# Extra constant products on TensorE in four waits of a one-core decoder, and one gather two batches earlier in its queue

## The chip, the core and the metric

One core of a Trainium2 chip runs the whole program. The metric is the device time of one execution in microseconds (us); smaller is better. Engines are named as in the profile: PE (TensorE, PEld its weight loads), DVE (VectorE), ACT (ScalarE), POOL (GpSimd), SP (SyncE, which issues DMAs).

## The reference

A two-layer decoder on 32 sequences of 128 tokens with 128 features. Every sublayer is followed by a residual sum and a layer norm.

```
layer 0: attention + MLP, cross-attention, a mixture of 8 experts (top 2)
layer 1: x4 = norm(x3 + experts)         # joined at the start of the decode phase
         x5 = norm(x4 + causal attention with rotary embedding (16 heads of 8))
         for t in 0..127:                # gated recurrence over the context
             r = decay * r + k[t] * v[t];   inp = (q[t] * r) @ Wi.T + bi
             gate = sigmoid(inp @ Wg.T + bg)
             state = tanh((gate * state + (1 - gate) * inp) @ A.T + inp @ Bm.T)
             out[t] = state @ Wo.T + bo
         x6 = norm(x5 + out);   x7 = norm(x6 + one of 8 experts (512 hidden, gelu))
```

## The kernel before, in words

The program is a row of phases, each a block in which every engine has its own instruction list; all engines meet in a barrier between two phases. Order between engines inside a phase is made by semaphores alone. Each list is written by a loop over ticks; `due(tick, offset)` says for which batch a step falls on this tick. Each engine runs its list in order, so a step that waits holds back all that stands behind it on its engine.

**`phase_decode`** (812 to about 1126 us of the span) runs ticks -25 to 148, four per batch (one per group of four heads, 128 units in all). For batch b, POOL gathers two expert rows by indirect DMA (L1574, `gather`), DVE joins them with x3 (L1797, L1832, on tick 4b-17) and takes mean and variance, POOL makes the reciprocal root (L1599), DVE makes x4 (L1840, tick 4b-13), PE transposes x4 (L1699, tick 4b-10), ACT copies it (L1744), PE projects q and k (L1679, tick 4b-8) and v, DVE multiplies with the rotary table (L1788), POOL adds and spreads (L1583, L1586, tick 4b-6), PE makes the scores (L1626, tick 4b-1), and on ticks 4b to 4b+3 DVE takes the maximum and subtracts it (L1771, L1775). ACT exponentiates, PE transposes into the bank `turned` (L1635) and weighs. At the end, on tick 4b+19, PE transposes x5 (L1714) and ACT copies it into `xT_all` (L1749).

POOL runs `gather(b)` on tick 4b-25, except `gather(4)`, which runs on tick -5, ahead of `gather(5)` and behind the rotary steps of batch 0. From b = 4 on, a gather waits until batch b-4 has been joined.

**`phase_recurrent`** (about 1127 to 1280 us) runs ticks -23 to 175. The 128 steps are cut into 16 spans of 8. For each span PE makes three products of 256 columns and more (L2038 input, L2042 gate, L2047 and L2050 drive), for span 0 on ticks -13, -10, -6 and -5. Per step there is a loop: PE product of 32 columns (L2008), ACT tanh (L2072), DVE product with the gate (L2130), back to PE. Every fourth tick a line of four steps goes on: three products (L2018, L2020, L2023), statistics, POOL's root, ACT x6 (L2091), transpose (L2014), logits (L2032), and for four lines the counts (L2055 to L2058). After the last line POOL scatters the last eight lines to memory (L1970) and DVE makes the tile table (L473 to L498).

**`phase_last`** (from about 1280 us) runs 40 tiles of 128 sorted rows: SP loads rows (L2264) and expert weights (L2272), PE transposes the rows (L2312), makes the hidden product (L2305) and the down product (L2320).

Of the kernel before, what the change touches and what calls it, by code (L numbers as in the profile page):

```python
# [14 lines left out]
P = 128  # L15
# [72 lines left out]
def stand_alone(eng, c):  # L88


    eng.sem_inc(c["stood"], 1)


def load_function(nc, c, function):
# [508 lines left out]
def phase_encode(nc, c, d, scr, keep, experts0, table0):  # L603

    with Phase(nc) as ctx:
# [6 lines left out]
        def bank(name):  # L612
# [3 lines left out]
        turned_bank, mix_bank, vec_bank, act_bank = bank("turned"), bank("mix"), bank("vec"), bank("act")  # L616
# [25 lines left out]
        scores_done, max_ready, bank_read, probs_ready, probs_turned, probs_t_ready, mixed, mix_copied = (  # L642
            sem("scores_done"), sem("max_ready"), sem("bank_read"), sem("probs_ready"), sem("probs_turned"),
            sem("probs_t_ready"), sem("mixed"), sem("mix_copied"))
# [111 lines left out]
        def _(pe):  # L756
# [58 lines left out]
            for tick in ENCODE_TICKS:  # L815
# [103 lines left out]
                if (i := group_at(tick, 69)) is not None:  # L919
# [8 lines left out]
                        if s < size:  # L928
                            nc.tensor.matmul(out, lhsT=c["tri"][:], rhs=r["any"][:, s, :], start=s == 0, stop=True)
                    last.then_inc(vec_written, 1)  # L930

        @block.scalar
        def _(act):
            def read(name, n):
# [500 lines left out]
def due(tick, offset):  # L1435

    n, rest = divmod(tick - offset, G)
    return n if rest == 0 and 0 <= n < BATCH else None


UNITS_ALL = BATCH * G


STEPS = 8
SPANS = P // STEPS
# [56 lines left out]
def phase_decode(nc, c, d, keep, scr, xT_all, experts1, recur):  # L1502
# [4 lines left out]
    with Phase(nc) as ctx:  # L1507
# [61 lines left out]
        def _(pool):  # L1569
            def gather(b):  # L1570
                if b >= 4:
                    pool.wait_ge(joined4, b - 3)
                for q in range(2):
                    nc.gpsimd.indirect_dma_start(out=y[q][b % 4][:], out_offset=None, in_=scr["expert_out0"],  # L1574
                                                 in_offset=bass.IndirectOffsetOnAxis(ap=route["out_rows"][:, b, q:q + 1], axis=0))\
                        .then_inc(gathered[b % 4], 16)

            for tick in TICKS:
# [21 lines left out]
                        .then_inc(rstd4_ready, 1)  # L1600
                if (b := due(tick, -26)) is not None and b in (12, 22):
                    pool.drain()
                if tick == -5:
                    gather(4)
                if (b := due(tick, -25)) is not None and b != 4:
                    gather(b)
                if tick == 104:
                    pool.drain()
# [7 lines left out]
        def _(pe):  # L1616
# [37 lines left out]
            for tick in TICKS:  # L1654
# [60 lines left out]
                if (n := due(tick, 7)) is not None:  # L1715
                    pe.wait_ge(mix_copied, n + 1)
                    if n:
                        pe.wait_ge(joined5, n)
                    else:
                        pe.wait_ge(halves_ready, 4)  # L1720
                    for k in range(G):
                        last = nc.tensor.transpose(vec_bank[:, k * P:(k + 1) * P], ot[n % 2][:, k * P:(k + 1) * P], c["ident"][:])
                    last.then_inc(mix_back, 1)

        @block.scalar
        def _(act):
# [150 lines left out]
def phase_recurrent(nc, c, d, scr, keep, e, xT_all, experts1):  # L1877
# [5 lines left out]
    with Phase(nc) as ctx:  # L1883
# [118 lines left out]
        def _(pe):  # L2002
            pe.wait_ge(e["loaded"], RECUR_LOADS)
            for tick in TICKS_RECUR:
# [47 lines left out]
                if (i := quad_at(tick, 32)) is not None:  # L2052
                    pe.wait_ge(hot_ready, i + 1)
                    at_votes = votes[:, COUNTED].rearrange("p (s e) -> p s e", e=EXPERTS)
                    nc.tensor.matmul(at_votes, lhsT=c["tri"][:], rhs=hot[:, 1:SLOTS + 2, :], start=True, stop=False)  # L2055
                    nc.tensor.matmul(at_votes, lhsT=c["ones"][:], rhs=hot[:, 0:SLOTS + 1, :], start=False, stop=False)
                    for s in range(2, SLOTS + 1):
                        last = nc.tensor.matmul(at_votes[:, s:SLOTS + 1, :], lhsT=c["ones"][:], rhs=hot[:, 1:SLOTS + 2 - s, :],  # L2058
                                                start=False, stop=s == SLOTS)
                    last.then_inc(counted, 1)  # L2060

        @block.scalar
        def _(act):
# [153 lines left out]
def phase_last(nc, c, d, keep, kept, e, sorted_rows, out, loaded):  # L2217
# [3 lines left out]
    with Phase(nc) as ctx:  # L2221
# [73 lines left out]
        def _(pe):  # L2295
            expert_of, experts = loader(pe, "down", "tile_expert", EXPERTS - 1), {}
            pe.wait_ge(keep["experts_loaded"], loaded)
            for tick in TICKS:
                if 0 <= (n := tick) < tiles:
                    pe.wait_ge(rowsT_ready, n + 1)  # L2300
# [193 lines left out]
```

## Time and profile before

| | |
|---|---|
| median of 3 runs | 1378.81 us (1376.04 to 1379.27) |
| the profiled execution | 1374.22 us, its span 1372.4 us |
| mean granted TensorE clock | 0.941 of full |
| busy | PE 87%, DVE 76%, ACT 63%, POOL 40% |

The rows further down are times from the start of the span. "PEclk" is the share of TensorE's full clock that was granted: 1.00 is 2.4 GHz and 0.50 is 1.2 GHz. Queue names such as SPq are the engine's issue of DMAs.

### The profile page before, as it was taken

Reading aid. Unit: us, or ns where it says so; the run is one execution under the profiler, and the core shown is the slowest. Engines: PE = TensorE matmul, PEld = TensorE weight load, DVE = VectorE, ACT = ScalarE, POOL = GpSimd, SP = SyncE. Lnnn points to the kernel's source line nnn. Section 1 sums busy time; section 2 is a strip of 40 time slices with the busy share of each in tenths; the row PEclk is TensorE's granted clock in tenths of the full one; section 3 lists DMA queues with packets and bytes.
Section 4 is the critical chain, followed back from the end, with each engine's and each line's share of the span. In section 5 each row is a group of like instructions: output and inputs, shape, how many; then the busy total and the mean of one; then the engine's idle time right before and its main releaser. Section 6 shows DMA issues by size and latency. Waiting matters only on the chain. (4 is left out here: it accounts for less than half of the span.)

```text
span 1372.4 us, 31512 instructions
## 1 busy us (share of the span) xinstructions
PE 1190.9 (87%) x10024; PEld 806.6 (59%) x10024; DVE 1042.1 (76%) x3169; ACT 863.6 (63%) x2470; POOL 552.7 (40%) x830
## 2 busy tenths in 40 slices
PE   3889999999999999988399977999999969997696
PEld 2456666666666666654266644555555537766696
DVE  3467888887888888876678867999999974665465
ACT  2578887878887878864256633666666654443464
POOL 1133333425353434442400026555556311556377
PEclk9899999999999999998599987999999988997798
DMA  6100000000000000000122222013100000000673
GB/s 267 50 15 11 17 15 21 29 17 27 16 30 17 28 17 17 15 13 13 56 71 82 82 66 95 23 38 94 28 24 19 1 3 1 17 17 21 180 209 90
DMA packets 71488, 63.51 MB, mean 46 GB/s; under 512 B 10510, under 2 KB 61586, under 8 KB 70688
## 3 DMA queue, kind: packets, MB, share of 16 engines
q1 hardware_dynamic: 63344, 46.33, 11.5%
q0 software_dynamic: 6400, 12.63, 2.9%
q10 hardware_dynamic: 1584, 2.54, 0.5%
q8 instruction: 85, 1.39, 0.4%
q14 instruction: 75, 0.61, 0.1%
HBM read 43.00 MB, written 18.98 MB: 45 GB/s over the span
## 5 line engine op out<-in xcount | busy, mean ns | idle before, releaser
L762 PE MATMUL e_bank_turned<-c_matrices,e_probs 128*128 128x128 f32 x1024 | 166.1, 286 | 16.0 <-ACT e_probs_t L995 8.7
L688 POOL TENSOR_TENSOR e_rstd<-e_var_eps,c_minus_half 128x1 f32<-128x1 f32 x128 | 70.7, 576 | 252.5 <-DVE e_var_eps L1036 252.2
L995 ACT ACTIVATE e_probs_t<-e_bank_turned 128x512 f32<-128x512 f32 x256 | 155.0, 605 | 16.1 <-PE e_bank_turned L762 14.6
L1123 DVE TENSOR_REDUCE e_neg_max<-e_bank_scores 128x4 f32<-128x512 f32 x160 | 109.6, 685 | 50.1 <-PE e_bank_scores L805 49.6
L762 PEld LDWEIGHTS e_bank_turned<-c_matrices,e_probs 128*128 128x128 f32 x1024 | 116.6, 145 | 39.8 <-issue 16.0
L772 PE MATMUL e_bank_mix<-e_probs_t,e_values 128*32 128x128 f32 x2048 | 113.6, 296 | 15.3 <-ACT e_probs_t L995 14.8
L954 ACT ACTIVATE e_probs<-e_scores,e_neg_max 128x128 f32<-128x128 f32 x384 | 123.3, 411 | 1.2 <-DVE e_neg_max L1159 1.2
L1752 ACT ACTIVATE d_probs_t<-d_bank_turned 128x512 f32<-128x512 f32 x128 | 77.4, 604 | 64.0 <-PE d_bank_turned L1635 64.0
L691 POOL TENSOR_TENSOR e_k_by_place<-e_q_k_k,c_matrices 128x512 f32<-128x512 f32 x64 | 66.6, 1040 | 105.3 <-DVE e_q_k_k L1167 105.3
L949 ACT ACTIVATE e_probs<-e_scores 128x512 f32<-128x512 f32 x128 | 82.1, 642 | 42.2 <-DVE e_scores L1156 41.6
L1734 ACT ACTIVATE d_probs<-d_scores 128x512 f32<-128x512 f32 x128 | 80.8, 631 | 42.4 <-DVE d_scores L1775 42.2
L1635 PE MATMUL d_bank_turned<-c_matrices,d_probs 128*128 128x128 f32 x512 | 82.2, 284 | 26.3 <-ACT d_probs_t L1752 21.3
L1635 PEld LDWEIGHTS d_bank_turned<-c_matrices,d_probs 128*128 128x128 f32 x512 | 55.5, 141 | 62.2 <-issue 53.5
L1775 DVE TENSOR_TENSOR d_scores<-d_bank_scores,d_neg_max 128x512 f32<-128x512 f32 x128 | 88.5, 692 | 4.4
L1156 DVE TENSOR_TENSOR e_scores<-e_bank_scores,e_neg_max 128x512 f32<-128x512 f32 x128 | 88.3, 690 | 3.4
L1771 DVE TENSOR_REDUCE d_neg_max<-d_bank_scores 128x4 f32<-128x512 f32 x128 | 87.5, 683 | 3.6 <-PE d_bank_scores L1626 3.6
L1574 POOL DMA_INDIRECT d_first<-scratch_expert_out,keep_out_rows x32 | 32.1, 1003 | 137.6 <-POOLq L85 131.7
L772 PEld LDWEIGHTS e_bank_mix<-e_probs_t,e_values 128*32 128x32 f32 x2048 | 41.2, 110 | 63.5 <-issue 34.4
L1325 PE MATMUL m_wide<-up,m_rowsT 128*128 x144 | 76.2, 612 | 0.4 <-ACT m_rowsT L1390 0.4
L699 POOL DMA_INDIRECT scratch_sorted<-e_x,e_row_u x64 | 64.2, 1003 | 26.8 <-issue 14.3
L2072 ACT ACTIVATE n_states<-n_bank_drive 128x32 f32<-128x32 f32 x128 | 25.2, 197 | 69.8 <-PE n_bank_drive L2008 68.4
L1125 DVE TENSOR_TENSOR e_scores<-e_bank_scores,c_bias 128x512 f32<-128x512 f32 x96 | 65.7, 684 | 0.0
(322 smaller groups left out, 3238.0 us busy)
## 6 DMA issues: line engine op xcount, KB each, us to landing
streamed<-in_s_up SPq DMA_DIRECT2D x40, 258.0 KB, 2.9
m_rows<-scratch_sorted SPq DMA_DIRECT2D x72, 64.0 KB, 1.8
scratch_expert_out<-m_y SPq DMA_DIRECT2D x72, 64.0 KB, 1.5
f_rows<-scratch_sorted SPq DMA_DIRECT2D x40, 65.0 KB, 2.5
e_x_in<-in_x SPq DMA_DIRECT2D x32, 64.0 KB, 1.8
e_ctx_in<-in_ctx SPq DMA_DIRECT2D x32, 64.0 KB, 2.1
up<-in_m_wgv SPq DMA_DIRECT2D x1, 2048.0 KB, 7.7
up_b<-in_m_bgv SPq DMA_DIRECT2D x1, 2048.0 KB, 14.3
```

The lines of the kernel that those rows point to most:

```text
L762: last = nc.tensor.transpose(turned_bank[:, j * P:(j + 1) * P], pr[k % 3][:, j, :], c["ident"][:])
L772: last = nc.tensor.matmul(mix_bank[32 * j:32 * j + VC, g * P:(g + 1) * P], lhsT=va[att][n % 3][:, G * g + j, :], rhs=pt[k % 2][:, j * P:(j ...
L949: nc.scalar.activation(pr[k % 3][:], sc[k % 4][:], ACT.Exp).then_inc(probs_ready, 1)
L954: last = nc.scalar.activation(pr[k % 3][:, j, :], src[:, j, :], ACT.Exp, bias=nmax[k % 4][:, j:j + 1], scale=1.0)
L995: nc.scalar.activation(pt[k % 2][:], turned_bank[:], ACT.Copy).then_inc(probs_t_ready, 1)
L1123: nc.vector.tensor_reduce(nmax[k % 4][:], bank, AX.X, ALU.max, negate=True).then_inc(max_ready, 1)
L1156: nc.vector.tensor_tensor(sc[k % 4][:], bank, bcast(nmax[k % 4][:], P), ALU.add).then_inc(bank_read, 1)
L1635: last = nc.tensor.transpose(turned_bank[:, j * P:(j + 1) * P], pr[u % 3][:, j, :], c["ident"][:])
L1734: nc.scalar.activation(pr[tick % 3][:], sc[tick % 4][:], ACT.Exp).then_inc(probs_ready, 1)
L1752: nc.scalar.activation(pt[(tick - 1) % 2][:], turned_bank[:], ACT.Copy).then_inc(probs_t_ready, 1)
L1771: nc.vector.tensor_reduce(nmax[tick % 4][:], bank, AX.X, ALU.max, negate=True).then_inc(max_ready, 1)
L1775: nc.vector.tensor_tensor(sc[tick % 4][:], bank, bcast(nmax[tick % 4][:], P), ALU.add).then_inc(shifted, 1)
```

## The change

A helper `stream` multiplies the constant identity with the first columns of a constant weight matrix (fp32, as many columns as its output has) into a part of PSUM whose contents nobody needs. It signals nothing and waits for nothing. It is called on PE

- in the decode phase on ticks -21 to -5 (17 calls of 256 columns), and on ticks 132 to 148 (17 calls of 128 columns), ahead of which PE waits for the last copy out of the bank `turned`;
- in the recurrence on ticks -12, -11, -9 and -4 (128 columns), and from tick 114 to tick 175 (62 calls of 128 columns), ahead of which PE waits for the last gate;
- in the last phase three times with 512 columns ahead of the first tile.

Each call stands behind the other PE steps of its tick. Besides, POOL's `gather(4)` moves from tick -5 to tick -9, its place by the rule of the other batches.

```diff
+def stream(nc, c, out):
+    nc.tensor.matmul(out, lhsT=c["ident"][:], rhs=c["a_w1"][:, 0:out.shape[1]], start=True, stop=True)
...
-                if tick == -5:
-                    gather(4)
-                if (b := due(tick, -25)) is not None and b != 4:
+                if (b := due(tick, -25)) is not None:
                     gather(b)
...
+                if -21 <= tick < -4:
+                    stream(nc, c, turned_bank[:, 0:2 * P])
+                if tick == UNITS_ALL + 4:
+                    pe.wait_ge(probs_t_ready, UNITS_ALL)
+                if UNITS_ALL + 4 <= tick:
+                    stream(nc, c, turned_bank[:, 0:P])
...
+                if tick in (-12, -11, -9, -4):
+                    stream(nc, c, turned[:, 0:P])
+                if tick == P - STEPS - 6:
+                    pe.wait_ge(gate_ready, SPANS)
+                if tick >= P - STEPS - 6:
+                    stream(nc, c, front[:, 0:P])
...
             pe.wait_ge(keep["experts_loaded"], loaded)
+            for _ in range(3):
+                stream(nc, c, sums[1][:])
```

## Rows read from the trace of the kernel before

**Rows 1.** The page, section 2: granted clock in 40 equal slices.

```profile
PEclk9899999999999999998599987999999988997798
```

**Rows 2.** Windows: length, busy by PE, PEld, DVE, ACT, POOL, granted clock, DMA, GB/s.

```profile
812.00:832.50 20.50, 12.21 (x44) 7.94 (x45) 9.78 (x33) 1.39 (x5) 15.64 (x20) 0.50 0.21 58
...
1122.60:1143.10 20.50, 14.68 (x41) 10.72 (x42) 8.65 (x35) 5.12 (x18) 1.79 (x3) 0.50 0.01 3
1143.10:1252.30 109.20, 102.79 (x620) 75.32 (x618) 69.61 (x328) 52.75 (x232) 52.89 (x112) 1.00 0.04 13
1252.30:1286.40 34.10, 15.00 (x68) 13.04 (x69) 12.29 (x60) 7.93 (x31) 16.14 (x25) 0.50 0.33 90
```

**Rows 3.** Timeline of the decoder's fill: start, duration, engine, line, operation, count, idle before.

```profile
814.61 1.89 PE L1619 MATMUL d_bank_scores<-c_causal_bf,c_ident_bf 128*128 128x512 bf16 x4 [5.61 <-DVE d_values L1762]
...
820.25 0.48 PE L1699 MATMUL d_bank_act<-c_matrices,d_x 128*128 128x128 f32 x1 [3.75 <-DVE d_x L1840]
...
825.08 0.57 POOL L1599 TENSOR_TENSOR d_rstd<-d_var_eps,c_minus_half 128x1 f32<-128x1 f32 x1
825.62 0.71 POOL L1583 TENSOR_TENSOR d_q_k_rotated<-d_halves 128x256 f32<-128x256 f32 x1
...
826.42 1.06 POOL L1586 TENSOR_TENSOR d_k_by_place<-d_q_k_rotated,c_matrices 128x512 f32<-128x512 f32 x1
...
827.96 0.46 POOL L1596 TENSOR_TENSOR d_x_bo<-d_x,c_rows 128x128 f32<-128x128 f32 x1 [0.48 <-DVE d_x L1840]
...
830.60 0.96 POOL L1574 DMA_INDIRECT d_second<-scratch_expert_out,keep_out_rows  x1 [0.30 <-issue]
...
833.19 0.35 DVE L1797 SCALAR_TENSOR_TENSOR d_sub<-d_first,keep_weights,d_x 128x128 f32<-128x128 f32 x1 [4.10 <-issue]
...
834.26 0.74 DVE L1840 TENSOR_SCALAR d_x<-d_sub,d_mean_var,d_rstd 128x128 f32<-128x128 f32 x1
...
835.53 0.68 DVE L1771 TENSOR_REDUCE d_neg_max<-d_bank_scores 128x4 f32<-128x512 f32 x1
```

**Rows 4.** Timeline of the decoder's end and the recurrence's start.

```profile
1124.95 0.48 PE L1714 MATMUL d_bank_act<-c_matrices,d_x 128*128 128x128 f32 x1 [1.99 <-DVE d_x L1827]
1125.46 0.39 ACT L1749 ACTIVATE xT_all<-d_bank_act 128x128 f32<-128x128 f32 x1 [2.07 <-PE d_bank_act L1714]
...
1127.00 0.61 DVE L2157 TENSOR_TENSOR n_held<-r_mem,xT_all 128x256 f32<-128x256 f32 x1 [1.35 <-PEq L85]
...
1127.76 1.19 PE L2038 MATMUL n_bank_front<-n_held,r_wi 128*128 128x256 f32 x2 [2.34 <-DVE n_held L2157]
...
1133.08 0.20 ACT L2072 ACTIVATE n_states<-n_bank_drive 128x32 f32<-128x32 f32 x1 [1.46 <-PE n_bank_drive L2050]
```

**Rows 5.** Timeline of the recurrence: the ninth tanh, an input product at full clock.

```profile
1143.84 0.20 ACT L2072 ACTIVATE n_states<-n_bank_drive 128x32 f32<-128x32 f32 x1 [0.49 <-PE n_bank_drive L2008]
...
1154.22 0.70 PE L2038 MATMUL n_bank_front<-n_held,r_wi 128*128 128x256 f32 x2
```

**Rows 6.** The line of the tanh between 1144 and 1245 us.

```profile
L2072 ACT ACTIVATE n_states<-n_bank_drive x106: 197/197/198, 1143.8 to 1244.9; 128x32 f32<-128x32 f32 x106
```

**Rows 7.** Timeline: tanh of steps 120 and 127, the last scatter, the last phase's head.

```profile
1251.85 0.20 ACT L2072 ACTIVATE n_states<-n_bank_drive 128x32 f32<-128x32 f32 x1 [0.85 <-PE n_bank_drive L2008]
...
1260.28 0.20 ACT L2072 ACTIVATE n_states<-n_bank_drive 128x32 f32<-128x32 f32 x1 [0.60 <-PE n_bank_drive L2008]
...
1274.35 0.96 POOL L1970 DMA_INDIRECT scratch_sorted<-n_x,n_row_u  x1 [0.30 <-issue]
...
1280.67 2.84 SPq L2264 DMA_DIRECT2D f_rows<-scratch_sorted  x5
...
1282.53 0.99 PE L2312 MATMUL f_turned_rows<-c_matrices,f_rows 128*128 128x128 f32 x2 [14.57 <-DMA f_rows<-scratch_sorted]
```

**Rows 8.** Timeline of the last phase: four 128-column products at half and full clock.

```profile
1283.34 2.08 PE L2305 MATMUL f_hidden<-f_rowsT,streamed 128*128 128x128 f32 x8
...
1355.17 1.06 PE L2305 MATMUL f_hidden<-f_rowsT,streamed 128*128 128x128 f32 x8
```

## The prediction

> **What bounds the kernel now.** I read the granted clock first, because nearly all that is added is PE work that nobody uses. The page shows full clock but for dips near 820 to 840, 1130 and 1250 to 1286 us [rows 1]. Windows put edges on them: half clock from 812.0 to 832.5, from 1122.6 to 1143.1 and from 1252.3 to 1286.4 us, full clock between the last two [rows 2]. The change puts its products into just these places. Then I asked in each place what the path hangs on. Four answers.
>
> In the decoder's fill it is not PE. DVE stands still for 4.10 us before it joins batch 4 at 833.19; the second gather of batch 4 started on POOL only at 830.60 and took 0.96 [rows 3]. In the same in-order list DVE's first maximum (unit 0) stands behind that join and starts at 835.53; it needs the scores of batch 0 too, but they had 6 us: POOL's spreading ended at 827.5 (826.42 + 1.06), and PE's product from it takes 2 us. The decoder then runs on DVE (busy over nine tenths), so a shift of that first maximum shifts the whole phase.
>
> At the recurrence's start it is PE: input, gate and drive products of span 0 form a chain with ACT and DVE from 1127.76 to the first tanh at 1133.08 [rows 4], and then the step loop runs. Nine tanhs later it is 1143.84 [rows 5]. In the bulk 106 tanhs start within 101.1 us, 0.963 a step [rows 6].
>
> At its end steps 120 to 127 take from 1251.85 to 1260.28 [rows 7], at half clock [rows 2].
>
> In the last phase PE works without a break once the first rows land, 1282.53 [rows 7]; it is slow until 1286.4 [rows 2].
>
> **Price of a product.** Four 128-column fp32 products take 1.06 us at full clock and 2.08 at half [rows 8]: 0.265 and 0.52 each, with the tail of the last one in it. Back to back I take 0.22 and 0.44 for 128 columns, twice that for 256, four times for 512; the other end is 0.265 and 0.52.
>
> **The gather.** It is two indirect DMAs; with their gaps 1.3 us each, 2.45 in all, and both sides of the move are on POOL. Before, POOL does root(2) 825.08 +0.57, rotation 0.71, spreading 1.06, bias(2) 0.46, root(3), then gathers 4 and 5 [rows 3]. After it, gather 4 starts at about 825.85 and its second half ends near 828.05; rotation and spreading end near 829.95; bias and root(3) end near 831.0. The data are there 1.6 us after the second half ends (830.60 + 0.96 to 833.19 before), at 829.7, so the next late thing is not the gather but root(3), which DVE's x4(3) needs. From x4(3) to the first maximum DVE takes 1.27 (834.26 to 835.53) [rows 3]. First maximum 831.0 + 1.27 = 832.3 instead of 835.5: **-3.3 us**. Scores of batch 0 now start when the spreading is done, 829.95, and take 1.1 to 2.1 us, done by 832.0 at the latest; covered. Moving past: rotation(0), bias(2), root(3) go 2.4 us later, gather 5 and rotation(1) stay within 0.5 us of their old time, since the same work is only reordered. Batch 5's join comes six us later than that; POOL has slack again. Bounds: -4.1 (the whole wait) to -2.
>
> **Products in the fill.** PE starts at 814.61 with 1.89 us of masks [rows 3], then 11 products of 256 columns stand before the transpose of x4(0), which ran at 820.25. A dense start at 1282.53 had its clock raised at 1286.4, 3.9 us later [rows 2, 7]; so here at about 818.5. To then 2.3 products are done, the other 8.7 take 0.44: the transpose starts near 822.3, 2.0 late. Two more stand before the projection, which ends near 824.4; DVE's rotary product (0.7 us) then ends near 825.2 instead of just before 825.62, where POOL took it up [rows 3]. POOL now wants it only at 828.05: about 3 us of cover. Cost **0**; if PE stayed at half clock, 11 x 0.87 would put the transpose at 826, the projection's end near 830, the first maximum back at about 835.3, and the gather's gain would be gone. PE idles from about 832.4 to 834.5 afterwards, so I don't count on full clock on ticks 0 to 4; if it holds, up to -0.7.
>
> **The decoder's end.** The products on ticks 132 to 142 lie in PE's waits for DVE and ACT; the last transpose waits for x5(31) at 1124.95 and I have PE free at 1124.5 by adding eleven times 0.22 to 0.265. Behind the transpose stand six products (ticks 143 to 148), 1.5 us, until about 1126.8. Before, the phase's last work was ACT's copy, 1125.46 + 0.39 = 1125.85, and the next phase started at 1127.00 [rows 4]. If the barrier waits for PE's array: **+0.95**. Bounds 0 (only PE's sequencer counts) and +3 (half clock).
>
> **The recurrence's start.** Three products of 256 columns stand in the chain; one took 1.19 at half clock [rows 4] and 0.70 at full [rows 5]: 3 x 0.49 = **-1.5**. Steps 0 to 8 took 1143.84 - 1133.08 = 10.76; eight at 0.963 are 7.70: **-3.1**. The products on ticks -12, -11 and -9 lie under ACT's and DVE's work on 256 columns (held, of this kind, takes 0.61); the one on tick -4 may hold the first step by 0.15: **+0.15**. With the barrier: -3.5. Bounds: +1 (clock not up) and -4.6.
>
> **The recurrence's end.** Seven steps took 8.43 us [rows 7], at 0.963 they would take 6.74: -1.7. Three line products stand between the last states and the last statistics: 3 x 0.26 saved, one added product of 0.22 in between: -0.5. Against that, 14 steps (114 to 127) carry a product of 0.22 to 0.265 each. PE is modelled as busy for 102.8 of 109.2 us there [rows 2], so the room is thin; ticks with three line products or a logits product have none, and these are about half: 7 x 0.15 = +1.0. Bounds 0 and 14 x 0.265 = +3.7. Sum **-1.2**. Behind step 127 the end hangs on POOL's scatters (the last at 1274.35) [rows 7], which start when the last x6 is there. The seven products between the last logits and the counts take 1.5 us and lie in PE's wait for ACT and six DVE steps, my estimate 1.5 us or a little more. Thirty-two more end near 1275, ahead of the barrier, before which the last phase's first DMA came at 1280.67.
>
> **The last phase's head.** PE is free at about 1280.0, my estimate: just ahead of SP's first DMA at 1280.67, which first loads its row numbers. It has been idle for 5 us by then, so at half clock. Three products of 512 columns: raised after 3.9 us, 1283.9, when 2.2 are done; the rest 0.7 us: 1284.6, 2.1 behind the rows. From there full clock. Before: 3.9 us at half clock from 1282.53, worth 1.95 us: like a start at 1284.5 at full clock. **0**; bounds -1.9 (full clock from the start) and +1.5.
> The Trainium skill (TensorE: Matmul & The Clock Gate, Part 1) says the moment of the rise is not tied to the kernel but runs free; by that this term differs from execution to execution within these bounds, and no single trace can show it.
>
> **Sum.** -3.3 + 0 - 3.5 - 1.2 + 0 = -8.0 us. Against the profiled execution: 1374.2 to 1366.2. That execution lies 4.6 us under the median of the runs; against the median: **1370.8 us**.
>
> **Rivals.**
> (a) The gather's gain is eaten: another DVE or POOL step is late instead, or POOL stays behind through ticks 0 to 8. For it: DVE's x4 takes 0.74 us beside POOL's rotation in the fill, twice what it takes alone; against it: POOL 40% busy over the kernel. Only the ends' -4.7: 1374.1. Chance 0.13.
> (b) The clock falls at the decoder's end before the products can hold it. Between 1118 and 1120 us PE has little but transposes, and tick 132 comes only at 1120. Then the products themselves run at 0.44 and shift the last transpose by about 2 us, until the rise near 1125: -8.0 + 2 = -6.0, 1372.8. Against it: the clock was still full until 1122.6. Chance 0.15.
> The Trainium skill (same page, Part 4: PE-mode transpose) says transposes do not count as busy in the same way; by that rule this rival would be the likelier. The trace does not bear it out strongly: full clock through 110 units of the decoder, in which about half of PE's instructions are transposes.
> (c) The products hold the clock, but all in-order costs come at their upper bound (steps 114 to 127 +3.7, barrier +2, head +1.5), or the clock is raised late at both ends: about -1, 1377.8. Chance 0.14.
> (d) Slower: the products do not raise the clock, and PE works through them at half clock in program order. Fill -0.2; decoder's end: last transpose 2.8 late, six products 3.1 instead of ACT's 0.9, +5; step loop 14 x 0.3 = +4; counts 7 x 0.44 = 3.1 in a wait of about 1.6, +1.4; the 32 products behind them end near 1283, +3; head +1: about +14, 1393. It decides itself by whether a run of such products counts as activity; against it, the dense products from 1282.53 did raise the clock. A milder form (half clock only in the recurrence's end) gives +4. Chance 0.07.
>
> **How the numbers follow.** Forecast 0.51 (1368 to 1373.5). Between the cases the likeliest is 1370.8. The range 1366.0 to 1378.5 takes in (a), (b), (c) and the bounds at which fill, head and start all go well; (d) and a little on the other side are left out. A measurement can tell some 0.3% (4.1 us) from no change: under 1374.7 is faster. Forecast, (b) and half of (a) lie there, with a part of (c): 0.77. Same 0.15. Slower 0.08.
>
> **What would show it.** DVE's wait before the join of batch 4 shrinks from 4.1 to about 1 us and the first maximum comes at 832 to 833. Granted clock 1.00 from 818 to 832 and through 1120 to 1145 and to 1275. First tanh about 4.5 us after the next phase's first DVE product instead of 6.1; eight steps in under 8 us. Steps 114 to 127 in 13.5 us or less. First row transpose of the last phase about 2 us after its rows have landed. Wrong would be: the first maximum still near 835, a clock of 0.50 anywhere between 1123 and 1260, steps of 1.2 us.

## The result and the profile after

The changed kernel takes 1369.71 us (median of 9 runs, 1365.88 to 1372.51), the kernel before 1376.49 us in its 9 runs beside them (1373.35 to 1379.27). The ratio is 0.9943, 95% interval 0.9928 to 0.9957, or 5.9 to 9.9 us less. The profiled execution took 1370.15 us (span 1368.4), that of before 1374.2 (span 1372.4). The time forecast was 1370.8.

The page of the changed kernel: busy time of the engines and the granted clock in 40 slices. The holes of [rows 1] at the decoder's end and the recurrence's end are gone, the one in the decoder's fill (slice 21) is not.

```profile
PE 1203.6 (88%) x10230; PEld 821.6 (60%) x10230; DVE 1041.3 (76%) x3169; ACT 862.0 (63%) x2470; POOL 554.3 (41%) x830
...
PEclk9899999999999999998599998999999999999998
```

Windows of the changed kernel over the stretches of [rows 2] (us, busy time and count of each engine, granted clock, DMA share, GB/s), first the decoder's fill, then both ends of the recurrence and the last phase's head.

```profile
810.30:815.30 5.00, 2.60 (x7) 1.52 (x8) 2.50 (x10) 0.00 (x0) 3.57 (x4) 0.50 0.35 93
815.30:829.80 14.50, 11.69 (x67) 9.53 (x66) 7.90 (x28) 1.39 (x5) 11.86 (x17) 0.97 0.19 50
829.80:839.80 10.00, 8.24 (x38) 4.27 (x36) 8.42 (x18) 4.04 (x8) 9.01 (x12) 0.50 0.27 67
...
1120.60:1141.10 20.50, 15.97 (x97) 12.36 (x96) 11.02 (x44) 6.73 (x23) 2.87 (x6) 1.00 0.02 4
...
1249.00:1276.40 27.40, 22.16 (x163) 20.24 (x162) 12.59 (x60) 6.53 (x25) 16.02 (x25) 0.88 0.29 88
1276.40:1284.40 8.00, 6.85 (x40) 5.00 (x41) 0.00 (x0) 2.90 (x13) 0.00 (x0) 0.97 0.34 81
```

The clock rises near 816, some 6 us into the fill (PE worked for 2.60 of the first 5, then ran products), but falls again near 829.8 and is half for ten us: the scores of the next units run there. It falls once more behind the recurrence's end, near 1270, for 6.8 us. The forecast had it at full from 818 to 832 and to 1275.

Timeline of the changed kernel in the fill, the rows that answer to [rows 3] (start, us, engine, line, operation; in brackets the idle time before and what ended it):

```profile
824.06 0.98 POOL L1578 DMA_INDIRECT d_first<-scratch_expert_out,keep_out_rows  x1 [0.18 <-issue]
...
828.04 0.35 DVE L1805 SCALAR_TENSOR_TENSOR d_sub<-d_first,keep_weights,d_x 128x128 f32<-128x128 f32 x1 [1.30 <-issue]
...
828.30 1.14 PE L1628 MATMUL d_bank_scores<-d_k_by_place,d_q_k_rotated 32*128 32x512 f32 x8 [2.35 <-POOL d_k_by_place L1590]
...
828.67 0.61 POOL L1603 TENSOR_TENSOR d_rstd<-d_var_eps,c_minus_half 128x1 f32<-128x1 f32 x1
829.31 0.41 DVE L1848 TENSOR_SCALAR d_x<-d_sub,d_mean_var,d_rstd 128x128 f32<-128x128 f32 x1 [0.46 <-POOL d_rstd L1603]
...
830.24 0.68 DVE L1779 TENSOR_REDUCE d_neg_max<-d_bank_scores 128x4 f32<-128x512 f32 x1
...
838.07 2.07 PE L1628 MATMUL d_bank_scores<-d_k_by_place,d_q_k_rotated 32*128 32x512 f32 x8
...
840.21 0.69 DVE L1779 TENSOR_REDUCE d_neg_max<-d_bank_scores 128x4 f32<-128x512 f32 x1 [1.68 <-PE d_bank_scores L1628]
```

DVE waits 1.30 us at the join of batch 4 instead of 4.10, and is held next by POOL's root, as forecast. New is the pair at the end: scores that take 2.07 us at half clock and DVE idle for 1.68 behind them. PE had stood for 2.35 us before the first scores, and the clock fell behind that pause.

Timeline of the changed kernel where the decoder ends and the recurrence begins; it answers to [rows 4]:

```profile
1124.47 0.33 PE L1716 MATMUL d_bank_act<-c_matrices,d_x 128*128 128x128 f32 x1 [0.85 <-DVE d_x L1835]
1124.64 1.50 PE L96 MATMUL d_bank_turned<-c_matrices 128*128 128x128 f32 x12
1124.84 0.40 ACT L1757 ACTIVATE xT_all<-d_bank_act 128x128 f32<-128x128 f32 x1 [1.67 <-PE d_bank_act L1716]
...
1127.19 0.61 DVE L2171 TENSOR_TENSOR n_held<-r_mem,xT_all 128x256 f32<-128x256 f32 x1 [2.01 <-PEq L85]
...
1131.70 0.20 ACT L2086 ACTIVATE n_states<-n_bank_drive 128x32 f32<-128x32 f32 x1 [0.94 <-PE n_bank_drive L2058]
```

L96 is the added product; one of them is two records (x12 is six). They end at 1126.14, and the barrier opens behind them.

The tanh of steps 120 and 127 of the changed kernel and its last scatter, as in [rows 7]:

```profile
1248.43 0.20 ACT L2086 ACTIVATE n_states<-n_bank_drive 128x32 f32<-128x32 f32 x1 [0.85 <-PE n_bank_drive L2016]
...
1254.89 0.20 ACT L2086 ACTIVATE n_states<-n_bank_drive 128x32 f32<-128x32 f32 x1 [0.38 <-PE n_bank_drive L2016]
...
1269.27 0.96 POOL L1978 DMA_INDIRECT scratch_sorted<-n_x,n_row_u  x1 [0.30 <-issue]
```

And what follows on PE and on SP's queue:

```profile
1262.47 4.71 PE L96 MATMUL n_bank_front<-c_matrices 128*128 128x128 f32 x40
1267.42 0.36 PE L96 MATMUL n_bank_front<-c_matrices 128*128 128x128 f32 x1 [0.24 <-issue]
1268.85 0.35 PE L96 MATMUL n_bank_front<-c_matrices 128*128 128x128 f32 x1 [1.07 <-issue]
1270.31 0.37 PE L96 MATMUL n_bank_front<-c_matrices 128*128 128x128 f32 x1 [1.11 <-issue]
1271.73 4.66 PE L96 MATMUL n_bank_front<-c_matrices 128*128 128x128 f32 x21 [1.05 <-issue]
1277.45 2.81 PE L96 MATMUL f_sums<-c_matrices 128*128 128x512 f32 x6 [1.07 <-PEq L85]
1280.10 0.54 PE L2328 MATMUL f_turned_rows<-c_matrices,f_rows 128*128 128x128 f32 x2
```
```profile
1265.24 6.43 SPq L454 DMA_DIRECT2D scratch_sorted<-r_pad  x4
1271.78 1.94 SPq L1965 DMA_DIRECT2D streamed<-in_s_up  x4
1277.99 2.84 SPq L2278 DMA_DIRECT2D f_rows<-scratch_sorted  x5
```

The first 20 products behind the counts run at 0.24 us each; then PE stands more than a microsecond ahead of each record, waiting for nothing that the profile shows, and the rest runs at 0.44 (half clock). PE ends at 1276.39, 7.1 us after the last scatter, and the barrier waits for it (bridge_long_tail below shows that it does): rows are loaded 8.72 us after the last scatter instead of 6.32.

Every stage of the two profiled executions, each measured from the event before it, so that the column of differences adds up to that of the spans:

| stage | before | after | difference | forecast |
|---|---|---|---|---|
| start to the decoder's first DVE instruction | 812.21 | 810.30 | -1.91 | - |
| to the first maximum | 23.32 | 19.94 | -3.38 | -3.3 |
| to the maximum of unit 8 | 17.26 | 18.48 | +1.22 | 0 |
| to the maximum of unit 112 | 229.38 | 232.97 | +3.59 | - |
| to ACT's last copy | 43.29 | 43.15 | -0.14 | - |
| end of that copy to the next phase's first DVE work | 1.15 | 1.95 | +0.80 | +0.95 |
| the copy (0.39, 0.40) and that work's start to the first tanh | 6.47 | 4.91 | -1.56 | -1.35 |
| tanh of step 0 to step 8 | 10.76 | 7.76 | -3.00 | -3.1 |
| step 8 to 114 | 101.94 | 102.86 | +0.92 | - |
| step 114 to 127 | 14.50 | 12.57 | -1.93 | -0.7 |
| to the last scatter | 14.07 | 14.38 | +0.31 | -0.5 |
| to the first row load | 6.32 | 8.72 | +2.40 | 0 |
| to the first transpose | 1.86 | 2.11 | +0.25 | 0 |
| to the end | 89.87 | 88.30 | -1.57 | (in it) |

Four rows had to be explained: +1.22, +3.59 with +0.92, and +2.40. The column "before" is one trace; the runs below show which of its rows repeat.

### The profile page after: what moved, and what is told of

The parts are those of the page before. It is cut to its first block and busy times, and to the rows that moved or that the text cites. A ratio compares the mean times of both kernels' runs of the same rounds, so it can differ in the third digit from the quotient of the medians.

```text
span 1368.4 us, 31923 instructions
## 1 busy us (share of the span) xinstructions
PE 1203.6 (88%) x10230; PEld 821.6 (60%) x10230; DVE 1041.3 (76%) x3169; ACT 862.0 (63%) x2470; POOL 554.3 (41%) x830
```

## The experiments

The runs came in three groups, each with its own runs of the kernel before, on three different chips. First group: `again`, `gather_only`, `tail_cut`, `no_fill`; second: `before_again`, `bounds_only`, `tail_only`, `fill_bridge`; third: the rest. On which chip or chips the first pair of traces was taken is not on record. "Unit 8 at 38.42" means that its maximum starts 38.42 us after the decoder's first DVE instruction; the other distances named below are read from timelines as in the table.

**again**: the changed kernel unedited.

> The changed kernel once more, for a second trace. Theory A (the stretches of the first trace are the kernel's own): first maximum of the decoder about 19.9 us after the phase's first DVE work; batches of the decoder at 8.9 us each (before 8.83) and one stall of 0.8 us near unit 58; at the end of the recurrence PE's last products stretched to about 1276 us with waits of 1.4 us between single ones, and 8.7 us from the last scatter to the first row load. Theory B (chance of one execution): the batches at 8.83 and no stall, the last products done about 8 us after the counts. Time about 0.994 of before.

1370.20 us, ratio 0.9954 (0.9939 to 0.9970). Its trace repeats the changed kernel's stages: first maximum 19.86, unit 8 at 38.14 (38.42 in the first trace), 232.35 from unit 8 to 112, steps 8 to 114 in 102.84, row loads 9.07 after the last scatter. All four rows repeat. What does not repeat is the clock at the decoder's end:

```profile
1116.90:1120.30 3.40, 3.40 (x15) 3.17 (x16) 1.94 (x14) 0.90 (x4) 0.66 (x2) 0.50 0.00 0
```

Here it was half for 3.4 us, where the first trace held 1.00, and ACT's last copy came 43.60 us after unit 112 instead of 43.15. tail_cut and no_gather show the same dip and the same late copy (43.60, 43.61).

**gather_only**: the kernel before with the gather moved, no products.

```
-                if tick == -5:
-                    gather(4)
-                if (b := due(tick, -25)) is not None and b != 4:
+                if (b := due(tick, -25)) is not None:
```

> The kernel before with gather(4) on tick -9 and no added product. Theory A (the gather alone carries the fill's gain, PE was not late): first maximum 3.3 us earlier after the phase's start than before (20.0 instead of 23.3), ninth maximum about 2 us earlier since the scores of batch 1 still meet half clock; total -2 to -3 us, ratio 0.998 to 0.9985. Theory B (the move shifts the phase between DVE, PE and POOL, and the decoder's batches take 8.93 instead of 8.83 us): the gain is given back by unit 60 to 120, total 0 or up to +1 us.

1374.58 us, 0.9986 (0.9972 to 1.0000). That is 1.8 us less than the kernel before by the medians (0 to 3.9). First maximum at 19.94 as in the changed kernel, but unit 8 at 36.75, 1.7 us ahead of it. From unit 8 to 112 it takes 233.03, the long batches of theory B. Windows of its fill:

```profile
810.30:829.00 18.70, 9.11 (x31) 5.91 (x35) 9.99 (x35) 1.39 (x5) 14.96 (x19) 0.50 0.24 64
829.00:833.00 4.00, 4.00 (x21) 2.80 (x14) 3.60 (x9) 0.63 (x1) 3.41 (x5) 0.50 0.19 51
833.00:850.00 17.00, 14.08 (x133) 8.00 (x132) 16.19 (x33) 10.09 (x21) 12.90 (x17) 1.00 0.43 152
```

Without products the clock stays half through the fill, rises at 833 from PE's own work and is full just where the changed kernel's is half.

**no_fill**: the changed kernel without the products on ticks -21 to -5.

```
-                if -21 <= tick < -4:
-                    stream(nc, c, turned_bank[:, 0:2 * P])
```

> The changed kernel without the 17 products of the decoder's fill; the gather stays on tick -9. Theory A (they are useless: the first maximum hangs on POOL's root): first maximum again about 20 us after the phase's start, total equal to the changed kernel within 0.5 us. Theory B (they carry part of the gain): first maximum later by 0.5 us or more.

1367.78 us, 0.9940 (0.9920 to 0.9961). Unit 8 at 36.85, 1.3 to 1.6 us ahead of the three kernels with them (38.42, 38.14, 38.37). The fill's products cost about 1.5 us in the trace; the medians, 2.4 us apart in that direction, can't tell it alone.

**tail_cut**: the last 32 products, behind the counts, left out.

```
-                if tick >= P - STEPS - 6:
+                if P - STEPS - 6 <= tick < P + 16:
```

> The changed kernel with the products of the recurrence's end on ticks 114 to 143 only; the 32 of ticks 144 to 175, behind the counts, are left out. Theory A (those 32 end last in the phase, held up among the DMAs, and the barrier waits for them): from the last scatter to the first row load 6.3 us as before instead of 8.7, total 2 to 2.5 us under the changed kernel (ratio to before about 0.9925). Theory B (they cost nothing, something else held the barrier, as SP's weight loads 2.1 us behind the tile table): the same 8.7 us and no gain.

1369.54 us, 0.9945 (0.9928 to 0.9962): no gain. The row loads come 7.48 after the last scatter (8.72 and 9.07 with the products), but the head pays it back:

```profile
1274.65 4.80 PE L96 MATMUL f_sums<-c_matrices 128*128 128x512 f32 x6 [13.60 <-PEq L85]
1279.29 0.38 PE L2328 MATMUL f_turned_rows<-c_matrices,f_rows 128*128 128x128 f32 x2
```

After 13.6 us without work the three wide products take 4.80 instead of 2.81, and the first transpose stands 4.10 behind the row loads.

**before_again**: one profile of the kernel before, on the second chip.

> The kernel before once more, for a second trace. Theory A (moving the gather changed how the decoder's batches run): its batches between the fifth and the twenty-eighth take 8.83 us again, 229.4 us from the ninth to the 113th maximum, against 232.4 to 233.0 in the five traces with the moved gather. Theory B (the first trace of before was one execution's luck): 8.93 us and about 232.5.

1375.54 us, span 1373.8. First maximum 23.75, unit 8 at 42.31, steps 0 to 8 in 9.11 us where the first trace had 10.76; batches of four units 8.83 apart, steps 8 to 114 in 101.92. From unit 0 to unit 8 it takes 18.56 us, where the first trace had 17.26. The clock was half there in both, in the first trace for 6.8 us,

```profile
835.90:842.70 6.80, 4.10 (x20) 2.30 (x21) 6.59 (x14) 3.86 (x8) 5.02 (x8) 0.50 0.07 19
```

and in before_again for 10.2:

```profile
834.80:845.00 10.20, 6.93 (x30) 2.98 (x31) 7.42 (x18) 4.05 (x8) 7.78 (x11) 0.50 0.31 76
```

**bounds_only**: the kernel before with the products at the decoder's end and the recurrence's start. **tail_only**: with those at the recurrence's end alone.

```
+                if tick == UNITS_ALL + 4:
+                    pe.wait_ge(probs_t_ready, UNITS_ALL)
+                if UNITS_ALL + 4 <= tick:
+                    stream(nc, c, turned_bank[:, 0:P])
...
+                if tick in (-12, -11, -9, -4):
+                    stream(nc, c, turned[:, 0:P])
```

> The kernel before with the products of the decoder's end (ticks 132 to 148) and of the recurrence's start (ticks -12, -11, -9, -4) alone; the gather stays on tick -5. Theory A (they hold the clock from the decoder into the recurrence, and that is worth its own share): barrier 0.8 us later, first tanh 1.57 us sooner after the first work of the phase, eight steps in 7.8 instead of 10.8 us: -3.8 us, ratio 0.9972; clock 1.00 from the decoder's last units to step 120. Theory B (it needs the other products too): the clock falls near the barrier and less than 2 us is gained. Also: batches of 8.83 us if the gather's place sets them.

> The kernel before with the products of ticks 114 to 175 of the recurrence alone. Theory A (steps 114 to 127 gain 1.9 us, and the phase's end gives it back): steps in 12.5 instead of 14.5 us, from step 127 to the last scatter 0.3 us more, from the last scatter to the first row load about 8.8 instead of 6.3 us: sum +0.9 us, ratio 1.0 to 1.001. Theory B (the end is held by something of the head, the three wide products): 6.3 us there and a gain of 1.6 us.

bounds_only 1369.98 us, 0.9985 (0.9968 to 1.0002); tail_only 1369.45 us, 0.9986 (0.9970 to 1.0002), against 1371.34 for the kernel before in that group. In the traces bounds_only has the barrier at 1.95, the first tanh at 4.52 and eight steps in 7.75; tail_only has steps 114 to 127 in 12.56, the last scatter 14.38 later and the row loads 6.56 after that, with the same 32 products behind its counts that cost 2.4 us in the changed kernel. They save 1.4 and 1.9 us by the medians, at the edge of what the runs can tell: both intervals hold 1. From unit 0 to 8 they take 18.26 and 18.54 us, as before_again does.

**fill_bridge**: the fill's products carried on to tick 1 (in another bank).

```
-                if -21 <= tick < -4:
-                    stream(nc, c, turned_bank[:, 0:2 * P])
+                if -21 <= tick < 2:
+                    stream(nc, c, mix_bank[:, 0:2 * P])
```

> The changed kernel with the fill's products of 256 columns carried on to tick 1 (into another bank that is free till tick 2), so that PE does not pause between the projections and the first scores. Theory A (in the changed kernel the clock rose too early and fell again in that pause, so that the first units ran at half clock; the pause is the cause): clock 1.00 from about 5 us after the phase's start through the first units, fifth maximum at 29.0 and ninth at 36.8 instead of 29.9 and 38.4, -1.5 us against the changed kernel. Theory B (the products themselves hold up PE): ninth maximum at 38 or later although the clock is full.

1361.70 us, 0.9924 (0.9902 to 0.9947). One window now covers the fill to past unit 4:

```profile
815.20:838.50 23.30, 19.77 (x132) 14.25 (x134) 16.61 (x44) 5.80 (x14) 20.52 (x27) 0.99 0.24 58
```

Unit 8 comes at 36.00. PE still pauses before the first scores, but for 1.38 us instead of 2.35. And the recurrence's end is that of tail_only, not of the changed kernel:

```profile
1254.20 7.39 PE L96 MATMUL n_bank_front<-c_matrices 128*128 128x128 f32 x64
1267.05 5.46 PE L96 MATMUL f_sums<-c_matrices 128*128 128x512 f32 x6 [5.46 <-PEq L85]
1272.30 0.63 PE L2328 MATMUL f_turned_rows<-c_matrices,f_rows 128*128 128x128 f32 x2
```
```profile
1256.71 2.83 SPq L454 DMA_DIRECT2D scratch_sorted<-r_pad  x4
...
1267.59 1.88 SPq L2278 DMA_DIRECT2D f_rows<-scratch_sorted  x4
```

All 32 products (64 records) run through without a gap, 0.6 us past the last scatter; SP's four pad rows take 2.83 us, not 6.43. So that difference, like the batches of 8.83 us in this trace, might belong to the chip. The third group repeats the kernel on another one.

**bridge_again**: fill_bridge unedited. **no_gather**: the changed kernel with the gather back on tick -5, all products kept.

> The changed kernel with its decoder products issued from tick -21 through tick 1 instead of through tick -5 (the kernel of fill_bridge, repeated beside its two variants). Theory C (what the decoder's products give hangs on the clock staying up over the matmul unit's pause before the first scores): about 9 us under the kernel before, ratio 0.992 to 0.995; granted clock 1.00 from about 6 us after the first DVE instruction of the decoder, maximum of unit 8 about 36 us after it, where the changed kernel had 38.4. Theory S (the longer decoder batches, 8.93 against 8.83 us, and the recurrence's 102.85 against 101.94 us, belong to the execution and not to the moved gather): this kernel and the one with the gather in its old place show the same batch in this call, whichever of the two it is. Theory G (the moved gather makes them): 8.93 here and 8.83 there, though the first trace of this kernel had 8.83.

> The changed kernel with the gather of batch 4 issued on tick -5 again, all products kept. Theory A (gather and products are independent): first maximum 23.3 us after the first DVE instruction of the decoder instead of 19.9, about 3.3 us slower than the changed kernel. Theory B (with the gather late the products end far ahead of the first scores and the clock falls anyway, so the late batch is hidden less): the same 3.3 us at unit 0, and unit 8 at 42 us or more, 3 to 5 us slower. For the batch: 8.83 or 8.93 us as in bridge_again by theory S, 8.83 by theory G whatever bridge_again shows.

bridge_again: 1370.72 us, 0.9951 (0.9932 to 0.9971). no_gather: 1373.33 us, 0.9969 (0.9957 to 0.9981), first maximum 23.43, unit 8 at 41.83. Against the changed kernel's traces unit 0 is 3.5 us later and unit 8 3.4 to 3.7: theory A. Unit 8 stays just under the 42 that theory B wanted.

bridge_again has unit 8 at 36.49, as theory C said, but its clock did not hold. PE paused for 1.84 us before the first scores, and 1.1 us into them the clock was down for 3.4 us:

```profile
829.81 1.14 PE L1628 MATMUL d_bank_scores<-d_k_by_place,d_q_k_rotated 32*128 32x512 f32 x8 [1.84 <-POOL d_k_by_place L1590]
```
```profile
830.90:834.30 3.40, 3.40 (x17) 3.22 (x14) 3.26 (x8) 0.63 (x1) 2.90 (x4) 0.50 0.21 59
```

In bridge_no_head and bridge_long_tail the pause was 1.50 and 1.52 us, and the clock held.

bridge_again has the long batches (mostly 8.90 to 9.05, 232.85 us from unit 8 to 112 against 229.38) and 102.87 us for steps 8 to 114; and no_gather, whose gather is in the old place, has them too (232.51 and 102.85). Theory S holds, G falls: one kernel shows both, and both positions of the gather show the long one. What makes the batches long was not found: DVE's instructions are as long in both traces of this kernel, and its listed waits over 180 us of the decoder sum up to 4.7 and 4.3 us. In the recurrence of bridge_again DVE shows waits for nothing, which fill_bridge lacks altogether:

```profile
DVE n_gated L2144 <- issue: 1.4, 5, 0.3
```

Where the batches were long, PE's stalls behind the counts were there too, if the 32 products stood there: row loads 8.72 to 9.14 us after the last scatter in six such traces (the changed kernel's, again, no_fill, bridge_again, bridge_no_head, no_gather), 6.56 and 6.59 in the two of the second chip. Without these products they came 6.32 to 7.14 us after it (four traces of kernels that have neither them nor the head's).

**bridge_no_head**: bridge_again without the three wide products. **bridge_long_tail**: bridge_again with 32 more products behind the counts.

```
-            for _ in range(3):
-                stream(nc, c, sums[1][:])
```
```
                 if tick >= P - STEPS - 6:
                     stream(nc, c, front[:, 0:P])
+                if tick >= P + 16:
+                    stream(nc, c, front[:, 0:P])
```

> The kernel of bridge_again without the three wide products ahead of the last phase. Theory H (those products are worth their place only where the matmul unit ran up to the barrier; after its pause they run at half clock and stand 2.8 us in front of the first row transpose): where the products of the recurrence end near the last scatter, first transpose 1.9 us after the row loads instead of 4.7, the rest of the phase 90 us instead of 88.4, so 1 us faster than bridge_again to equal. Rival (the raised clock of the head is worth more than the delay): 1 to 1.5 us slower than bridge_again.

> The kernel of bridge_again with a second product on each of the 32 ticks from P + 16 on, so that the matmul unit runs some 3.7 us longer behind its last count. If it then ends 4.3 us after the last scatter, still ahead of the barrier (5.5 us after it at the earliest), the clock is held and the wide products take 1.4 to 2.8 us at full clock: first transpose about 2.1 us after the row loads, the phase 88.4 us, 1.5 to 2.5 us faster than bridge_again. Rival (the stalls of 1.07 us for one product seen in the changed kernel return and hold the barrier): row loads 9 us or more behind the last scatter instead of 6.6, no faster than bridge_again or up to 3 us slower.

bridge_no_head: 1371.02 us, 0.9954 (0.9937 to 0.9972), not to be told from bridge_again. Its trace has the first transpose 1.89 behind the row loads (2.10) and 90.26 us from there (88.65): where PE ran up to the barrier the head's products save 1.4 us. In fill_bridge, where PE had paused for 5.46, the sum of the two is 4.71 + 88.40 = 93.11, in tail_only without them 1.93 + 90.14 = 92.07: there they cost 1.0. Theory H in both halves, but by one pair of traces each; the medians (0.3 us apart) don't show it.

bridge_long_tail: 1376.45 us, 0.9992 (0.9979 to 1.0005), 5.7 us more than bridge_again. PE and SP in its trace:

```profile
1272.16 0.35 PE L96 MATMUL n_bank_front<-c_matrices 128*128 128x128 f32 x1 [1.13 <-issue]
1273.58 11.21 PE L96 MATMUL n_bank_front<-c_matrices 128*128 128x128 f32 x86 [1.08 <-issue]
1285.85 2.81 PE L96 MATMUL f_sums<-c_matrices 128*128 128x512 f32 x6 [1.06 <-PEq L85]
```
```profile
1266.96 5.86 SPq L454 DMA_DIRECT2D scratch_sorted<-r_pad  x4
...
1286.39 2.84 SPq L2280 DMA_DIRECT2D f_rows<-scratch_sorted  x5
```

PE ends 13.7 us after the last scatter (7.5 in bridge_again), the row loads follow at 15.27 (9.14): PE works 6.1 us longer and the row loads come 6.1 us later. The row loads move by as much as PE's end: the barrier waits for these products.

## Why the prediction was right, and where not

The time came within 1.1 us, and the range held it. But the base of the forecast, the median of three runs (1378.81), was 2.3 us above that of the nine beside the changed kernel. Against these the change gave -6.8 where -8.0 was forecast, and several terms of the sum were wrong and cancelled.

**The gather (-3.3)** was right in size and in mechanism, -3.38, with POOL's root as the next late thing. Over all traces the first maximum comes at 23.3 to 24.6 (five traces, mean 23.7) with the gather in its old position and at 19.8 to 20.0 (nine traces) with the moved one. no_gather gives the same from the other side. So rival (a) is out in the traces; by the medians gather_only gained 1.8 us (0 to 3.9), and what became of the rest of its traced gain is not shown.

**Products in the fill (0).** The step that failed is "3 us of cover": it asked only whether the products delay the projection (they don't), and did not price what the clock does on ticks 0 to 4. With the gather moved, unit 8 comes at 36.75 and 36.85 without the products and at 38.13 to 38.42 with them (three traces): they cost about 1.5 us. Without them the clock rises 22.3 to 22.8 us after the decoder's first DVE instruction, where the first scores and their successors are due, and stays. With them it rises 5.3 to 5.8 us after it, falls at 18.9 to 19.5, behind a pause of PE of 2.2 to 2.4 us, and is back at 29.2 to 29.7.

Against the kernel before this is a gain missed and not a loss. The +1.22 of the table stands against the one trace of four with a short stretch of half clock (6.8 us); the three others take 18.26 to 18.56 us from unit 0 to 8, the changed kernel 18.27 to 18.50. In the kernel before PE stands for 4.9 to 6.0 us before the first transposes of `turned`, waiting for ACT, and the clock falls in that wait. The moved gather takes the wait away, which is worth another 1.6 us up to unit 8 (16.80 and 16.82 in gather_only and no_fill), and the products give just this back. With the gather in its old place they cost nothing (no_gather 41.83; without them 40.58, 42.09, 42.31, 42.81).

With the products carried on to tick 1, unit 8 comes at 36.0 to 36.5 (four traces), 1.6 to 2.4 us earlier than in the changed kernel and 0.3 to 0.9 earlier than with no products at all. PE's pause was 1.4 to 1.8 us there, and the clock held in three traces and fell for 3.4 us in the one with the longest. That fits the pause as the cause of the fall, but does not show it alone: the same products also give PE more work behind the scores.

**The decoder's end (+0.95)** was right: +0.80 in all ten traces that have the products. Rival (b) came true in part. In the changed kernel's own trace the clock was 1.00 from 1120.6 to 1141.1; in again, tail_cut and no_gather it fell for 3.4 us amid the added products and was back before the barrier. The last copy was 0.45 us late in just these three (43.14 to 43.16 in the seven others), not the 2 us of rival (b). The Trainium skill (TensorE: Matmul & The Clock Gate, Part 4: PE-mode transpose) says that transposes don't count as busy in the same way. The traces don't bear it out as a rule for a mixture: from 843 to 1118 us of the kernel before, the clock was 1.00 though over two fifths of PE's instructions were transposes (715 of 2450 records; the fp32 products leave two records each). For the dips no run separates transposes from idle time, since in again PE was also busy for only 1.96 of the 3.40 us before.

**The recurrence's start** came out as forecast in the pair (-1.57 to the first tanh, and -3.00 of -3.1 for eight steps), but the second figure flattered it. Steps 0 to 8 took 10.76 in the first trace of the kernel before, 9.11, 8.50 and 9.10 in the three other traces without the products (before_again, gather_only, tail_only; mean 9.37). With them they took 7.75 in six traces and 8.87 to 9.11 in four (mean 8.25). The term is -1.1 on average, not -3.1: the step that failed is the reading of 10.76, one slow execution, as the price of that stage. Windows of bridge_again show why it isn't always 7.75:

```profile
1131.30:1134.30 3.00, 2.21 (x12) 1.49 (x10) 1.77 (x6) 1.65 (x7) 0.00 (x0) 1.00 0.00 0
1134.30:1138.30 4.00, 3.94 (x17) 3.60 (x17) 0.92 (x5) 0.94 (x4) 0.00 (x0) 0.57 0.00 0
1138.30:1142.00 3.70, 3.37 (x19) 2.19 (x18) 1.91 (x9) 1.46 (x6) 1.08 (x3) 1.00 0.00 0
```

The clock dips three us after the first tanh, in a PE that was busy 3.21 of 4.30 and 2.21 of 3.00 us before. The same code dips in bridge_again and not in fill_bridge. The four traces with 8.87 to 9.11 are the four that dip here; those with 7.75 do not. The Trainium skill (same page, Part 1) says that the moment of the rise isn't tied to the kernel; these traces fit it: in the fill of the same code the rise came 5.3 to 5.8 us after the first DVE instruction, and the dip here comes in some executions and not in others. So the four products of this stage, with the gaps that they leave, don't hold the clock in every execution.

**The recurrence's end (-1.2 with the step costs).** Steps 114 to 127 gained 1.93, where -1.7 and +1.0 had been set: the 14 products in the step loop cost nothing that the traces show. Here the first trace was a cautious base: the four traces without these products took 14.50, 14.56, 15.24 and 15.37 (mean 14.9), the ten with them 12.52 to 12.57, so -2.4 on average. To the last scatter +0.31 instead of -0.5. Together -1.6. But **the 32 products behind the counts (0)** were another failed step: "thirty-two more end near 1275, ahead of the barrier". The pace of 0.22 that I took held for the first twenty only; then came the stalls, and 1.05 + 0.37 us a record for three of them, then half clock. +2.4 us against the first trace, 2.2 against the mean of the four without (6.8), 1.2 us of which (tail_cut, 7.48) come back when they are left out, and are lost again in the head. tail_cut is as fast as the changed kernel because the two are coupled: without PE work up to the barrier, the wide products run at half clock.

**The head (0)** gained 1.3 net, since PE came to it without a pause, for the reason just told. The two terms together are +1.1, where 0 stood. From the last scatter to the end of the kernel, the four traces with neither the 32 products nor the head's took 98.1 to 99.8 us (mean 98.8), the six with the 32 and the head's 99.1 to 99.9. So in the traces these 35 products together bring nothing. The changed kernel without both sets was not run.

**Sum.** The rows which the change can have touched add up to -6.6: all but the first, and but the two (+3.59 and +0.92) that no_gather and the fill_bridge pair lay to the execution. By the medians, again and the changed kernel itself lie 6.2 and 6.8 us under the kernel before, so the forecast of -8.0 was 1.2 to 1.8 too good. With the means of all traces in place of the first pair the sum is about -7: the start of the decoder up to unit 8 -3.6, its end -0.2, the barrier +0.8, the first tanh -1.6, eight steps -1.1, steps 114 to 127 -2.4, the last scatter +0.3 and all behind it +0.7. That the sum came out near is partly luck: the eight steps were priced 2.0 us too high and the steps at the end 1.7 too low, and the two cancelled. The miss that is left is mostly the last scatter and what lies behind it, priced at -0.5 and measured at +1.0. These means mix three chips, so they are an estimate.

**No version that is clearly better.** fill_bridge was 9.6 us under the kernel before in one group of runs and 6.8 in the other; the intervals of both contain the changed kernel's 0.9943. no_fill (0.9940) is as good without its 17 products. That a bridge over the fill is faster than the changed kernel is what the traces say (1.6 to 2.4 us at unit 8), not what the medians prove.

**Still open.** Whether the kernel before has the long batches on the first and third chip is argued only: it was timed there 5.0 and 6.2 us above its median on the second chip, about what 3.5 and 0.9 us would give, but not profiled. What PE waits for in its stalls was not found, nor what decides in which execution the clock dips.

## What to carry to other kernels

A product that only holds the clock is worth its place if it lies within a wait and if what follows it has no pause of its own. In this fill the clock was raised early, PE then stood for 2.35 us, and the clock was half when the real work came. Put no such product behind the last real instruction before a barrier without counting it at its slowest price, for here the barrier waited for all of them. And price a stage at half clock from several executions, since one trace can be more than a microsecond from the mean in either direction.

## What the runs showed of the hardware

- Behind the counts PE stood again and again for 1.04 to 1.16 us before single records with nothing to wait for, on two chips, and SP's four pad rows took 5.9 to 6.4 us in the same stretch; on another chip 64 records ran without a gap and the pads took 2.8 to 3.1. The slow pads don't need the products: they took 5.18 in tail_cut, which has none there, and 3.53 in gather_only. The DMA share was 0.29 from 1249 to 1276 us of the changed kernel. What the two have in common was not found.
- The same kernel runs its decoder batches in 8.83 or about 8.95 us and the steps 8 to 114 in 101.9 or 102.9 us, by the execution and, in these runs, by the chip: all profiles of the first and third group have the long ones, all of the second the short ones; of the first pair, the kernel before had the short and the changed one the long. That is 4.5 us, two thirds of this change's gain, so traces from different chips can't be subtracted stage by stage without a repeat.
- In the fill of the changed kernel the granted clock fell to half near 829.8, after PE had stood from 825.94 to 828.30, and stayed there for 10 us although PE was busy for 8.24 of them. In the recurrence's start, where PE had gaps but was busy for three quarters of the time, the same program dipped to 0.57 in one execution and held 1.00 in another.
- The clock dipped to half for 3.4 us at the decoder's end in three of the ten traces that have the products there, in the recurrence's start in four others, and in neither place in three (the changed kernel's, bounds_only, fill_bridge).
